# A maximum in place of a leaky relu in one edge stage, and a product taken in two halves in one node stage

## What is computed

```python
src_h = h[src]
se = jnp.concatenate([src_h, eh], axis=-1)
msg = jax.nn.leaky_relu(se @ W_msg, 0.01)          # one value of 64 features per edge
q = jnp.concatenate([qrh, qeh], axis=-1) @ W_q / temp
k = se @ W_k
att = jnp.sum(q * k, axis=-1)
e = jnp.exp(att - m[dst])                          # m: maximum of att over the edges of a node
alpha = e / segment_sum(e, dst)[dst]
agg = segment_sum(alpha[..., None] * msg, dst)
...
x = _layernorm(x + layer2(x, ...))
```

## Time and profile before

| | us |
|---|---|
| median of 3 runs | 9136.01 |
| range of the runs | 9131.16 to 9145.02 |
| the profiled execution | 9133.93 |
| its span, first to last instruction | 9132.2 |
| GpSimd busy | 6676.1 (73%) |
| VectorE busy | 5454.6 (60%) |
| ScalarE busy | 2476.6 (27%) |
| TensorE busy | 1872.5 (21%) |
| second half of node stage 1, from 4680 to 4787 | 107 |
| edge stage 2, from 4787 to 6830 | 2043 |

### The profile page before, as it was taken

One profiled execution on the slowest core, in us unless ns is written; L12 is line 12 of the kernel. 1 busy time (PEld: TensorE's weight loads), 2 busy tenths in 40 slices (PEclk: granted clock), 3 DMA queues, 4 the chain that ended last, 5 costly groups with the idle time before them and its releaser, 6 DMA issues. The chain is left out here.

```text
span 9132.2 us, 36460 instructions
## 1 busy us (share of the span) xinstructions
PE 1872.5 (21%) x4249; PEld 957.9 (10%) x4249; DVE 5454.6 (60%) x6299; ACT 2476.6 (27%) x2302; POOL 6676.1 (73%) x6997
## 2 busy tenths in 40 slices
PE   3000000000200000000054444444434222222224
PEld 1000000000200000000032222222213101010104
DVE  5365656565657777777727777777766333333335
ACT  0122222232523232323231111111114333333333
POOL 6777777776777777777647777777765777777776
PEclk6555555555555555555576666676667656565656
DMA  8233333333123333333225555555542333333332
GB/s 354 82 108 109 108 109 108 111 106 106 31 91 106 107 108 105 111 102 113 86 79 183 179 175 186 178 175 186 178 138 71 115 121 115 121 115 123 113 123 82
DMA packets 384127, 1146.63 MB, mean 126 GB/s; under 512 B 163424, under 2 KB 194682, under 8 KB 362128
## 3 DMA queue, kind: packets, MB, share of 16 engines
q1 hardware_dynamic: 127984, 676.77, 19.7%
q0 software_dynamic: 249696, 445.02, 17.7%
q10 hardware_dynamic: 6336, 23.79, 0.7%
HBM read 736.78 MB, written 408.32 MB: 125 GB/s over the span
## 5 line engine op out<-in xcount | busy, mean ns | idle before, releaser
L783 POOL DMA_INDIRECT pair<-pair_table,edge_ix x1512 | 1480.5, 979 | 460.6 <-issue 460.6
L783 POOL DMA_INDIRECT g<-x_table,edge_ix x1512 | 1427.9, 944 | 460.8 <-issue 460.8
L783 POOL DMA_INDIRECT hidden<-hidden_table,edge_ix x1512 | 1426.7, 944 | 460.8 <-issue 460.8
L783 POOL DMA_INDIRECT qv<-qv_table,edge_ix x1484 | 1400.2, 944 | 452.2 <-issue 452.2
L921 ACT ACTIVATE edge_sums<-edge_val 128x1904 f32<-128x1904 f32 (+3 forms) x220 | 1112.4, 5056 | 459.8 <-DVEq L1535 459.8
L1340 PE MATMUL edge_pair_ps<-w_e,edge_eh_t 128*128 128x384 f32 x1568 | 916.4, 749 | 1101.4 <-DVEq L1393 1086.3
L864 ACT ACTIVATE edge_bank<-edge_weight_arg 128x112 f32<-128x112 f32 (+3 forms) x169 | 38.6, 228 | 3215.0 <-DVE edge_decay_arg L855 3215.0
L911 DVE TENSOR_TENSOR_SCAN edge_val<-edge_bank,edge_val 128x464 f32<-128x464 f32 (+1 forms) x715 | 687.6, 1032 | 358.0 <-ACT edge_val L1497 353.9
L1489 PE MATMUL edge_e_ps<-w_nodes,edge_ea_t 128*128 128x512 f32 x784 | 476.4, 773 | 1465.3 <-DVEq L1529 1456.6
L1528 DVE TENSOR_TENSOR hidden<-hidden,edge_e_ps 128x3584 f32<-128x3584 f32 x55 | 213.8, 3888 | 842.5 <-DMA hidden<-hidden_table,edge_ix 791.9
L1124 DVE TENSOR_TENSOR edge_product<-edge_k_ps,qv 128x896 f32<-128x896 f32 x112 | 185.7, 1658 | 690.7 <-DMA qv<-qv_table,edge_ix 683.4
(11 more groups left out here) (430 smaller groups left out, 5730.9 us busy)
## 6 DMA issues: line engine op xcount, KB each, us to landing
sums<-edge_sums SPq DMA_DIRECT2D x56, 1848.0 KB, 7.1
edge_q_in<-in_edge_attr_q SPq DMA_DIRECT2D x56, 1792.0 KB, 9.6
sums<-edge_sums SPq DMA_DIRECT2D x55, 1792.0 KB, 6.3
sums<-edge_sums SPq DMA_DIRECT2D x56, 1008.0 KB, 4.0
sums<-edge_sums SPq DMA_DIRECT2D x55, 924.0 KB, 4.1
edge_k<-k_edges SPq DMA_DIRECT2D x56, 896.0 KB, 4.6
edge_bond<-in_edge_attr SPq DMA_DIRECT2D x56, 896.0 KB, 8.3
edge_eh_t<-in_edge_attr_t SPq DMA_DIRECT2D x56, 896.0 KB, 4.7
```

Of the source, the lines that this page charges most:

```text
L783: e.indirect_dma_start(self.gather_into(u, j), None, self.gather_from, bass.IndirectOffsetOnAxis(ap=now[:, j:j + 1], axis=0))\
```

## The change

In edge stage 2, ScalarE copies the message times 0.01 (`damp`) into `values`, transposed, as soon as VectorE has signalled with the new semaphore `joined` that all pieces of the chunk are in `msg`. In ScalarE's order `damp` stands ahead of the chunk's exponentials. VectorE waits for it (`damped`) after the softmax' arguments, takes the maximum of `msg`, read transposed, and `values` into `values`, and multiplies `values` in place by the weights. L1404 and L1407 are replaced by these two. The last chunk's two parts are changed likewise.

In node stage 1, `project` and `take_x` work on a group in two halves of two tiles (the second is empty in the groups of 4 and 3 rows), each half with its own `x_taken`, so that the copy of the first half can start when its two tiles are multiplied, and the next group's first half when these two banks are copied. SyncE waits for both before it stores a group. On ScalarE the order becomes take_x of the first half, square, take_x of the second half, light, move_x, root.

```diff
@@ edge_phase_2
+        joined, damped = ph.sem("joined"), ph.sem("damped")
...
         @block.scalar
         def _(e):
+            def damp(i, b, to, now=slice(0, J), more=0):
+                e.wait_ge(joined, at(i, 2, 1 + b + more))
+                e.activation(to, msg[:, now, :].rearrange("p j d -> p d j"), ACT.Copy, scale=0.01).then_inc(damped, 1)
+
             with e.Fori(0, ph.rounds - 1) as i:
                 for b in (0, 1):
+                    damp(i, b, ph.values(b)[:, 0, :, :])
                     ph.exponentials(e, i, b, decay)
                     ph.lay_out(e, i, b)
...
             def chunk(i, b):
                 for k in range(per):
                     weigh(i, b, k)
+                e.sem_inc(joined, 1)
                 e.sem_inc(ph.rows_free[b], 1)
                 e.sem_inc(ph.attr_free[b], 1)
                 ph.carry_values(e, i, b)
                 ph.running_softmax(e, i, b)
-                e.scalar_tensor_tensor(msg[:, :, :], msg[:, :, :], 0.01, msg[:, :, :], ALU.mult, ALU.max)
+                values = ph.values(b)[:, 0, :, :]
+                e.wait_ge(damped, at(i, 2, 1 + b))
+                e.tensor_tensor(values, msg[:, :, :].rearrange("p j d -> p d j"), values, ALU.max)
                 e.drain()
                 ph.wait_decay(e, i, b)
-                e.tensor_tensor(ph.values(b)[:, 0, :, :], msg[:, :, :].rearrange("p j d -> p d j"),
-                                bcast(ph.weight[:, 0, :], 1, FD), ALU.mult)
+                e.tensor_tensor(values, values, bcast(ph.weight[:, 0, :], 1, FD), ALU.mult)
...
@@ node_phase_1
+        x_taken = [ph.sem(f"x_taken{half}") for half in (0, 1)]
+        halves_of = lambda g: (range(0, min(2, firsts[g])), range(2, firsts[g]))
+        upto = lambda g, half: sum(1 for k in range(g) for part in halves_of(k) if part) + half + 1
...
             for g in range(groups):
-                e.wait_ge(x_taken, g + 1)
+                for half in (0, 1):
+                    after(e, x_taken[half], sum(1 for k in range(g + 1) if halves_of(k)[half]))
...
-            def project(g):
+            def project(g, half):
+                now = halves_of(g)[half]
+                if not now:
+                    return
                 e.wait_ge(x_moved, g + 1)
-                after(e, x_taken, g)
-                for k in range(firsts[g]):
+                after(e, x_taken[half], sum(1 for k in range(g) if halves_of(k)[half]))
+                for k in now:
                     last = e.matmul(pair_banks[:, k, :], x_t[g % 2][:, k, :], p.w2_x, start=True, stop=True)
                 last.then_inc(x_done, 1)
...
-            in_turn(groups, (1, turn_back), (8, turn_x), (10, project), per=4)
+            in_turn(groups, (1, turn_back), (8, turn_x), (10, lambda g: project(g, 0)), (11, lambda g: project(g, 1)), per=4)
...
-            def take_x(g):
-                n, one = ph.sizes[g], firsts[g]
-                e.wait_ge(x_done, g + 1)
+            def take_x(g, half):
+                now, n, to = halves_of(g)[half], ph.sizes[g], pair_out[g % outs]
+                if not now:
+                    return
+                e.wait_ge(x_done, upto(g, half))
                 after(e, stored[g % outs], 16 * (g // outs))
...
-                    (11, take_x), per=4)
+                    (11, lambda g: take_x(g, 0)),
+                    (12, lambda g: take_x(g, 1)), per=4)
```

More of the change, by code:

```diff
@@ L1351, in _ @@
             i = ph.rounds - 1
+            damp(i, 0, ph.values(0)[:, 0, :, :])
             ph.exponentials(e, i, 0, decay)
             ph.lay_out(e, i, 0)
+            damp(i, 1, ph.by_head(ph.part(0))[:, 0, 0:FD, :], ph.columns(0))
             ph.exponentials(e, i, 1, cut_decay(0), 0)
@@ L1356, in _ @@
             ph.lay_out_cut(e, lambda to, of: e.activation(to, of, ACT.Copy))
+            damp(i, 1, ph.by_head(ph.part(1))[:, 0, 0:FD, :], ph.columns(1), 1)
             ph.exponentials(e, i, 1, cut_decay(1), 1)
@@ L1422, in part_of_last @@
                 ph.running_softmax(e, i, 1, now.start, now.stop)
-                m = msg[:, now, :]
-                e.scalar_tensor_tensor(m, m, 0.01, m, ALU.mult, ALU.max)
+                values = ph.by_head(ph.part(more))[:, 0, 0:FD, :]
+                e.wait_ge(damped, 2 * i + 2 + more)
+                e.tensor_tensor(values, msg[:, now, :].rearrange("p j d -> p d j"), values, ALU.max)
                 e.drain()
                 ph.wait_decay(e, i, 1, more)
-                e.tensor_tensor(ph.by_head(ph.part(more))[:, 0, 0:FD, :], msg[:, now, :].rearrange("p j d -> p d j"),
-                                bcast(ph.weight[:, 0, now], 1, FD), ALU.mult)
+                e.tensor_tensor(values, values, bcast(ph.weight[:, 0, now], 1, FD), ALU.mult)
                 e.drain()
@@ L1974, in node_phase_1 @@
         stored = [ph.sem(f"pair_stored{u}") for u in range(outs)]
-        x_turned, x_moved, x_done, x_taken = ph.sem("x_turned"), ph.sem("x_moved"), ph.sem("x_done"), ph.sem("x_taken")
+        x_turned, x_moved, x_done = ph.sem("x_turned"), ph.sem("x_moved"), ph.sem("x_done")
+        x_taken = [ph.sem(f"x_taken{half}") for half in (0, 1)]
+        halves_of = lambda g: (range(0, min(2, firsts[g])), range(2, firsts[g]))
+        upto = lambda g, half: sum(1 for k in range(g) for part in halves_of(k) if part) + half + 1
         w_k, w_q = ph.sb("w_k", [P, FD]), ph.sb("w_q", [P, FD])
@@ L2092, in move_x @@
                 e.wait_ge(x_turned, g + 1)
-                after(e, x_done, g - 1)
+                after(e, x_done, upto(g - 1, -1))
                 e.activation(x_t[g % 2][:, 0:n, :], x_ps[:, 0:n, :], ACT.Copy).then_inc(x_moved, 1)
-            def take_x(g):
-                n, one = ph.sizes[g], firsts[g]
-                e.wait_ge(x_done, g + 1)
-                after(e, stored[g % outs], 16 * (g // outs))
-                made = pair_banks[:, 0:one, :].rearrange("p k (u f) -> p k u f", u=2)
-                pairs = n // 2
-                last = e.activation(pair_out[g % outs][:, 0:2 * pairs, :].rearrange("p (k u) f -> p k u f", u=2),
-                                    made[:, 0:pairs, :, :], ACT.Copy)
-                if n % 2:
-                    last = e.activation(pair_out[g % outs][:, n - 1, :], made[:, pairs, 0, :], ACT.Copy)
-                last.then_inc(x_taken, 1)
+            def take_x(g, half):
[3 more added lines that the diff above has]
+                e.wait_ge(x_done, upto(g, half))
+                after(e, stored[g % outs], 16 * (g // outs))
+                made = pair_banks[:, now.start:now.stop, :].rearrange("p k (u f) -> p k u f", u=2)
+                pairs = min(n // 2, now.stop) - now.start
+                if pairs:
+                    rows = slice(2 * now.start, 2 * (now.start + pairs))
+                    last = e.activation(to[:, rows, :].rearrange("p (k u) f -> p k u f", u=2), made[:, 0:pairs, :, :],
+                                        ACT.Copy)
+                if pairs < len(now):
+                    last = e.activation(to[:, n - 1, :], made[:, pairs, 0, :], ACT.Copy)
+                last.then_inc(x_taken[half], 1)
             in_turn(groups, (2, move), (4, keep), per=2)
```

## The result

| | before | after |
|---|---|---|
| median | 9138.49 us | 9212.68 us |
| range, 4 runs each | 9131.16 to 9145.02 | 9212.10 to 9217.41 |
| span of the profiled execution | 9132.2 us | 9210.7 us |
| ratio after / before | | 1.0083, 95% interval 1.0065 to 1.0100 |

What follows compares the result with a forecast made beforehand. GpSimd's gathers were taken to bound edge stage 2. From 9133.9 us, +102.6 for longer holds, +1.0 for the last chunk and -13.6 for node stage 1 gave 9223.9; 2.1 more for the median made 9226 us, range 9160 to 9250.

Steps and rivals of the forecast that it cites:

- The bound: Edge stage 2 lasts as long as its gathers on GpSimd, one per 1.25 us; GpSimd never waits for buffers.
- The rule of the hold: Two-SBUF-input VectorE instruction stretches the first gather starting in it by its length, less that gather's start offset, less 0.13 us.
- Rival (a): Edge stage 2: the transposed maximum holds up no gather, so the kernel gets faster, 9071 us; chance 0.07.
- D: Length of the holding VectorE instruction; for edge stage 2's new maximum taken as 3.18 us.
- (c): Edge stage 2: the maximum takes 2.03 us, +0.72 per chunk, 9163 us; chance 0.04.
- (d): Edge stage 2: the maximum takes 4.33 us, +3.02 per chunk, 9289 us; chance 0.06.
- The start of the maximum: Edge stage 2: the maximum starts 3.46 us after the chunk's last reduction, 1.95 later than L1404.
- Rival (b): Edge stage 2: maximum starts over 0.36 us later than forecast, missing the next gather; +0.94 per chunk, 9175 us; chance 0.12.
- n and the stretch: Time from instruction start to held gather's start, 0.93 us before, 0.23 (n') after; stretch per chunk 0.96 to 2.82, +102.6 us.
- The covers: Edge stage 2: VectorE's tail, 1.95 us later per chunk, and the exponentials queued behind ScalarE's Copy stay hidden.
- Node stage 1: Halved groups shorten light to light by 1.05 us in 13 full-size groups: -13.6 us.
- Rival (e): Node stage 1: the halves gain nothing since both engines run in a fixed order; 9240 us, no separate chance given.

Runs made afterwards that it cites:

- e1: Kernel before with the edge stage 2 change alone, node stage 1 as before: 10423.0 us against 10437.7, ratio 0.9985.
- e4: Changed kernel with the old in-place scalar_tensor_tensor where the maximum stands, product reading transposed: 10448.1 us, ratio 1.0012 to the kernel before.
- e9: Kernel before with the edge stage 2 change alone, the same kernel as e1 run again: 9228.75 us against 9131.95, ratio 1.0106.
- e2: Kernel before with the node stage 1 change alone: 10420.3 us, ratio 0.9983.
- e10: Kernel before with the node stage 1 change and the old leaky relu cut into four instructions of 7 columns: 9068.16 us against 9131.95, ratio 0.9929.

## Why the prediction was right, step by step

**The bound.** Right, and the whole argument hangs on it: GpSimd's idle time in the stage stayed 460.7 us of issue. e1 shows the same edit costing nothing once this is not so. The prediction named GpSimd waiting for freed rows as a sign of being wrong, but gave it no chance of its own, and nothing in the profile of before warned of it.

**The rule of the hold.** Right in form, except at its edge: the first gather that starts in the instruction is let through when it starts within 0.04 us (e1, e4). The constant is 0.127 us for the contiguous read, as read (0.13), and 0.166 for the transposed one. Rival (a), that the transposed maximum doesn't hold, is refuted by L1416's rows. The inference in the Trainium skill (SBUF — State Buffer, Who interferes with whom) that tensor_tensor leaves descriptor generation alone does not carry over to these gathers: 55 are held by one, 2.65 us each. Whether it is wrong is open. The same section says that an instruction with two SBUF inputs contends with a GpSimd instruction that reads SBUF, and these gathers read their indices from the SBUF tile `edge_ix`; no run here separates the reading of indices from the writing of descriptors. So that page did not speak for rival (a) as plainly as the prediction has it.

**D.** Taken 3.18 between bounds of 2.03 and 4.33; measured 3.207. The argument that a second SBUF input adds nothing to the transposed form held within 0.03 us. Rivals (c) and (d) fall with it.

**The start of the maximum.** Taken 3.46 after the last reduction; measured 3.36. The Copy (3.26 to 3.27) and the hand-over back (0.03) were as read; ScalarE starts 0.06 after the reduction's end, not 0.16. The mis-sized term is this one: I took it from a VectorE instruction (L829) behind a drain and two increments, and ScalarE waits for the first of the two alone. Rival (b) would not have needed a start 0.36 later, as I wrote, but one at most 0.19 later, since a gather within 0.04 us is already let through. The start came 0.10 earlier instead, and no chunk fell on the next gather (n between 0.22 and 0.46). That none did is in part luck: at the forecast start the earliest gather would have started about 0.12 us into the maximum, near the edge. Rival (b) deserved more than its 0.12, though its 9175 lay inside the range.

**n and the stretch.** Forecast n' = 0.23 and 2.82 us; measured 0.365 and 2.68, the means of the 54 chunks with a full maximum. Of the difference in n, 0.10 is the earlier start and 0.03 the n of before, which was 0.96 and not 0.93. With c = 0.166: 3.207 - 0.365 - 0.166 = 2.68. With the last chunk's shorter hold that gives the mean of 2.65, so +1.72 a chunk instead of +1.87, and 145.8 - 51.0 = 94.8 in place of 102.6.

**The covers.** Held. GpSimd never waited for freed buffers in after, and VectorE still sits 319 us ahead of pieces for rows to land (315 in before, 306 in e9). The exponentials run beside the maximum.

**The stage's end.** Forecast +1.0. It is not so that the gathers have run out by then: the last chunk's first part, a maximum of 1152 elements and 2.12 us, holds one for 1.30 us (0.77 in before), which is within the 145.8; from the last gather of the stage to the first of the next node stage it is 25.0 us before and 26.0 after.

**Node stage 1.** Forecast -13.6, measured -18.8, between the bounds of -20.2 and +1.4 that I gave. The loop itself came out at 5.24 us against 5.30. What was mis-sized is the clock. I left the groups at a fallen clock as they were, and in after there are none. There were three of them and not four (the fourth long interval is the first full group's, in which the clock rises); so that bound was 4.9 us and not 6.6, and all of it came in: the other 13.9 are 1.11 in each of ten intervals and 0.9 in each of three at the two ends. I had argued from the clock that was granted to the old pattern of work, while the change itself changed the pattern: TensorE's 4.2 us of matmuls for a group now lie in 5.24 us and not in 6.35, and in none of the eleven traces with the node part does the clock fall in this row of groups. Rival (e) is refuted.

**The sum.** Forecast 102.6 + 1.0 - 13.6 = +90.0 on the profiled execution; measured +78.5. The stretch is 7.8 less and the node stage gave 5.2 more, each of known cause, and both errors went the same way. Against these 13.0 stand 1.5 that the sum didn't have: 1.1 in the gathers of the first two chunks and 1.4 behind the stage, less 1.0 by which this execution was ahead before the first changed instruction.

## What to carry to other kernels

Ask of each long VectorE instruction with both inputs in SBUF whether a GpSimd gather starts inside it. Where GpSimd is the bound, such a gather waits for the instruction's end, and work that was moved to a third engine can cost more through a longer such instruction than it saves. Two cures were tried. Cutting the instruction is shown in gathers and time: four quarters that take 2.22 us held 2.6 us in the stage where one of 2.02 us held 51.0. One input in PSUM is shown in the gathers alone (none held), not in the time. And before a ratio is carried to another run, look at whether the engine that made it is still the one that never waits.

## What the runs showed of the hardware that I had not expected

The same program ran at 9132 to 9138 us and at 10,438 to 10,501 us, each steady within a group of runs, at nearly the same mean granted clock (0.577 and 0.571 for one kernel). In the longer runs VectorE waited for TensorE's pieces, which in e2 came 8.6 us (median of the 72 waits) after their first matmul's start, and gathers in edge stage 1 were longer too: 574 of 1512 in e1 take over 0.985 us, 14 in before, and in the loop there none of VectorE's instructions over 0.3 us has two SBUF inputs. GpSimd's groups by line of e1 and e9 for the edge stage 1:

```profile
L783 POOL DMA_INDIRECT g<-x_table,edge_ix x1512 | 1590.1, 1052 | 507.5 <-issue 507.5
...
L783 POOL DMA_INDIRECT g<-x_table,edge_ix x1512 | 1427.2, 944 | 460.8 <-issue 460.8
```

There that costs 163 us of gathers and 47 of issue in one stage. The cause isn't settled by anything here.

Four two-input instructions of 448 elements in a row let a gather through between them, with 0.11 us of delay in the chunk shown and 0.09 on average over the 28 that were held (e10); the hold is not taken over from one to the next.

A gather that starts within 0.04 us of such an instruction is let through, and then it is the VectorE instruction that is longer: in e4 the 22 of these chunks have a scalar_tensor_tensor of 2.08 us where the others have 2.02. The transposed maximum of e1 shows no such difference (3.21 in both).
